# Score matmuls over 128 columns of keys instead of 72 in the cross attention of layer 0

## The reference, cut to what matters

```
q_c = q @ W_dq ;  kv_c = kv @ W_kvc ;  k_rope = rope(kv_c @ W_kr)
scores = (einsum(q_nope, k_nope) + einsum(q_rope, k_rope)) * scale
good = (k_ids <= seg) & (k_ids >= seg - 8)
attn = softmax(where(good, scores, -1e30))
out = einsum(attn, v) @ W_o
```

## Time and profile before

| | before |
|---|---|
| median of 3 runs | 1418.46 us |
| lowest and highest run | 1415.54 and 1429.39 us |
| span of the profiled execution | 1416.6 us |
| PE busy in it | 1114.3 us (79%) |
| weight loads busy | 825.4 us (58%) |
| DVE busy | 764.6 us (54%) |

### The profile page before, as it was taken

The page is one execution under the profiler, slowest core; times in us unless marked ns, Lnnn a source line. Parts: engine busy times, 40 slices in busy tenths (PEclk is TensorE's granted clock), DMA queues, the critical chain, the costliest instruction groups (busy, mean ns, idle before and its releaser), DMA issues.

```text
span 1416.6 us, 14414 instructions
## 1 busy us (share of the span) xinstructions
PE 1114.3 (79%) x5107; PEld 825.4 (58%) x5111; DVE 764.6 (54%) x1025; ACT 469.9 (33%) x719; POOL 479.1 (34%) x331
## 2 busy tenths in 40 slices
PE   3899977879999887686769689699733478489996
PEld 2543454547777766575657678544521367378885
DVE  6212122653344554998999995414697764533333
ACT  2111122552111634464446533333311132133331
POOL 5231212330000433465646560034454980011211
PEclk9799986975555897788878889899955555599999
DMA  6576601220000114313231300102030000111110
GB/s 174 204 266 215 253 0 28 58 60 19 0 0 1 56 42 157 117 47 119 74 106 58 125 10 16 60 0 74 15 121 0 0 0 1 48 60 44 59 44 30
DMA packets 50448, 97.88 MB, mean 69 GB/s; under 512 B 6796, under 2 KB 26564, under 8 KB 47838
## 3 DMA queue, kind: packets, MB, share of 16 engines
q1 hardware_dynamic: 47198, 86.59, 18.4%
q0 software_dynamic: 3200, 10.62, 2.2%
HBM read 96.14 MB, written 1.05 MB: 69 GB/s over the span
## 4 chain that ended last, share of the span: by engine, by line
PE 58%; DVE 23%; issue 11%; ACT 4%; POOL 2%; SPq 0%; DMA 0%; POOLq 0%; DVEq 0%; ACTq 0%
PE banks L41 7%; PE banks L42 7%; PE banks L43 7%; PE banks L354 6%; PE banks L1794 4%; PE banks L1097 3%; PE banks L1096 3%; PE banks L2109 2%; PE banks L1424 2%; PE banks L1452 2%; DVE da_a L1357 1%; PE banks L1087 1%; PE banks L1806 1%; DVE da_s L1351 1%; DVE da_s L1341 1%
## 5 line engine op out<-in xcount | busy, mean ns | idle before, releaser
L155 POOL TENSOR_TENSOR w_low<-w_raw,w_high 128x1024 fp32r<-128x1024 f32 (+2 forms) x66 | 129.9, 1982 | 307.9 <-ACT w_high L151 307.8
L354 PE MATMUL banks<-cs_rows,cs_col 128*2 128x512 f32 x192 | 85.3, 594 | 0.2 <-DVE w_raw L318 0.2
L1642 POOL TENSOR_TENSOR tw_abs<-tw_abs,tw_w 128x2048 bf16<-128x2048 bf16 x12 | 49.0, 4083 | 95.0 <-DVE tw_abs L1635 95.0
L151 ACT CAST w_high<-w_raw 128x1024 fp32r<-128x1024 f32 (+2 forms) x66 | 53.4, 831 | 83.2 <-DMA w_raw<-in_L_attn_Wq 47.1
L2217 POOL TENSOR_TENSOR hf_hl<-hf_h,hf_hh 128x512 fp32r<-128x512 f32 x16 | 20.6, 1289 | 155.1 <-ACT hf_hh L2271 155.1
L1424 PE MATMUL banks<-da_k,da_q 64*128 64x128 f32 x256 | 35.7, 396 | 38.4 <-issue 38.4
L1424 PEld LDWEIGHTS banks<-da_k,da_q 64*128 64x128 f32 x256 | 33.9, 288 | 41.5 <-issue 41.5
L41 PE MATMUL banks<-da_xT_high,w_high 128*128 128x512 f32 x128 | 52.5, 410 | 6.3 <-POOL w_low L155 5.7
L929 DVE SCALAR_TENSOR_TENSOR wa_s<-banks,wa_bd 128x288 f32<-128x288 f32 x16 | 7.3, 457 | 86.4 <-PE banks L1097 86.4
L41 PE MATMUL banks<-hf_xhh,w_high 128*128 128x512 f32 x128 | 51.7, 404 | 0.0
L669 POOL TENSOR_TENSOR wa_kr<-wa_kr,wa_tab 128x288 f32<-128x288 f32 x8 | 6.4, 794 | 132.8 <-ACT wa_kr L724 132.5
(11 more groups left out here) (419 smaller groups left out, 3160.7 us busy)
## 6 DMA issues: line engine op xcount, KB each, us to landing
cs_rows<-in_ctx SPq DMA_DIRECT2D x16, 1536.0 KB
tw_raw<-in_L_ffn_w_gate_up SPq DMA_DIRECT2D x32, 256.0 KB, 3.7
w_raw<-in_L_xattn_W_o SPq DMA_DIRECT2D x8, 512.0 KB
w_raw<-in_L_attn_Wq SPq DMA_DIRECT2D x8, 512.0 KB
w_raw<-in_L_attn_Wk SPq DMA_DIRECT2D x8, 512.0 KB
w_raw<-in_L_attn_Wv SPq DMA_DIRECT2D x8, 512.0 KB
w_raw<-in_L_attn_Wo SPq DMA_DIRECT2D x8, 512.0 KB
tw_raw<-in_L_ffn_w_proj SPq DMA_DIRECT2D x16, 256.0 KB, 3.8
```

What stands on the lines that cost most here:

```text
L151: self.nc.scalar.copy(self.wh[k][:, 0:cols], self.raw[k][:, 0:cols]).then_inc(self.split_hi[k], 1)
L155: self.nc.gpsimd.tensor_tensor(self.wl[k][:, 0:cols], self.raw[k][:, 0:cols], self.wh[k][:, 0:cols].bitcast(F32), ALU.subtract).then_inc(s ...
L354: ins = nc.tensor.matmul(out, self.col[:, h * self.HALF + r, :], self.rows[h][:, r, :], start=(h == 0 and r == 0), stop=False)
L1642: g.tensor_tensor(a, a, self.w[j][:, :], ALU.subtract).then_inc(self.d_ok, 1)
```

## The change

The score matmuls of a group stream 128 columns of keys: the group's own 72 and 56 of its neighbours. For the groups of rounds 0 to 14 the 128 columns begin at the group's own; for the last round, where nothing follows the last group, they end with the group's own (`key_offset` is then 56). A group's result takes 128 columns of the PSUM bank, four groups the whole bank of 512. DVE's first step reads from it the same 4 x 72 columns as before, now with gaps between the groups. All else stays: the number of instructions, the waits, the softmax, both kinds of transposes and the matmuls of L1110.

```
+    def key_offset(r):
+        return 0 if r < WindowAttention.G // 4 - 1 else P - WindowAttention.KEYS
...
-                ch(v.scalar_tensor_tensor(s[:, :, :], c.bank[:, r % 2, 0:4 * self.KEYS].rearrange("p (g k) -> p g k", g=4), X_SCALE,
+                own = slice(self.key_offset(r), self.key_offset(r) + self.KEYS)
+                ch(v.scalar_tensor_tensor(s[:, :, :], c.bank[:, r % 2, :].rearrange("p (g k) -> p g k", g=4)[:, :, own], X_SCALE,
...
+        flat = lambda t: t[:, :, :, :, :].rearrange("p m g j t -> p (m g j t)")
+
+        def wide(t, g):
+            at = g * K8 - self.key_offset(g // 4)
+            return flat(t)[:, at:at + P]
...
-                    out = c.bank[:, n, q * K8:(q + 1) * K8]
-                    nc.tensor.matmul(out, self.qa[:, 8 * g:8 * g + 8, :].rearrange("p t h -> p (t h)"), keys(self.kvcT, g), start=True, stop=False)
-                    ins = nc.tensor.matmul(out, self.qr[:, 8 * g:8 * g + 8, :].rearrange("p t h -> p (t h)"), keys(self.krT, g), start=False, stop=True)
+                    out = c.bank[:, n, q * P:(q + 1) * P]
+                    nc.tensor.matmul(out, self.qa[:, 8 * g:8 * g + 8, :].rearrange("p t h -> p (t h)"), wide(self.kvcT, g), start=True, stop=False)
+                    ins = nc.tensor.matmul(out, self.qr[:, 8 * g:8 * g + 8, :].rearrange("p t h -> p (t h)"), wide(self.krT, g), start=False, stop=True)
```

## The result

The changed kernel takes 1432.17 us at the median of 20 runs (1421.06 to 1444.76), the kernel before 1417.72 us at the median of 20 (1413.45 to 1430.24). The ratio is 1.0081 with a 95% interval of 1.0053 to 1.011: slower, by 7.5 to 15.6 us. Three of the changed kernel's 20 runs (1443.66 us and more) count as slow runs, and the ratio is of the others, whose median is 1429.21 us. The forecast was 1430.4 us, +0.84%, with 1410 to 1440 us as its range.

What follows compares the result with a forecast made beforehand. The score stage's ring of PE scores and DVE's chain was taken as the bound, at clock 0.50. Eight matmuls at 0.0933 us over 16 rounds add 11.9 us: 1418.5 + 11.9 = 1430.4 us, +0.84%, range 1410 to 1440 us.

Steps and rivals of the forecast that it cites:

- The ring: Score stage, each 9.10 us round: L1087 0.86 us, scores 4.88 us, DVE's chain 3.36 us; added score time lengthens all 16 rounds.
- One of two instructions shows its growth: Score matmul pairs: only the second PE instruction's 0.093 us shows; pair 0.63 to 0.73 us, 11.9 us over 16 rounds.
- Charging both instructions: Rival in the score pairs: both instructions show their growth, 23.9 us slower, 1442.4 us; chance 0.04.
- The load waits at a change of rows: Score loop: at each change between 128 and 64 contraction rows, the next load waits for the matmul before it.
- at every change of rows and nowhere else: Argument against 72 columns being slow as a shape: loads start 0.07 us before a matmul's end only at row changes.
- The gapped read costs nothing: DVE's first step, L929: reading 288 elements with gaps stays at 0.46 us; at most 3.6 us more in all.
- The clock stays at 0.50: Score stage: the granted clock stays 0.50 after the change, the stage taking 161 us.
- The rival that wider matmuls lift the clock: Score stage: denser PE streaming restores the full clock; 1382 us if throughout, 1406 us if half; chance 0.11.
- the break-even: Clock rival in the score stage: share of the stage at clock 1.00 that offsets the added columns, put at a quarter.
- Eight changes of rows a round: Score loop: all 8 matmuls of a round have a row change behind them, each showing 0.0933 us, 0.747 us a round.
- The range of 3.6 us for DVE's read: Upper bound for L929's gapped read, as if all 512 elements were read: 0.22 us a round; nothing was taken.
- The doubt whether the result would stand inside or outside 1%: Whole kernel: 11.9 us lies just within the 14.2 us limit; forecast's 0.80 split into 0.58 within and 0.22 slower.

## Why the prediction was right

The forecast rests on the stage, and there sum and rows agree: +11.9 us forecast, 161.59 - 149.66 = 11.9 us measured. That the whole kernel's median came within 2 us of the forecast is in part luck: the profiled execution came out 5.7 us under the span that was forecast (1422.8 against 1428.5 us), and single runs spread over 24 us.

**The ring.** Scores and DVE's chain alternate, and what the scores gain or lose shows in full. DVE's wait for them grew by 11.9 us, PE's idle time stayed at 0.58 us, and the stage grew by 11.9 us. This step held.

**One of two instructions shows its growth.** Predicted 0.72 us a pair and 9.85 us a round, measured 0.72 and 9.85. With 100 columns 9.47 was expected and 9.475 measured. Charging both instructions would have given 23.9 us. Once a pair, then, is shown. Which of the two instructions it is, is not. The prediction says the second, because the next load waits for its end, and this does not fit its own rows: from the second's start to the next load it is 0.35 us with 72 and with 128 columns, and the growth stands before that start, 0.28 us against 0.38 and 0.37 after the change. That the first one's growth hides behind the second load was argued only. Since the ends of matmuls in the trace are modelled, and both instructions of a pair always have the same columns, no run here separates the two. The sum does not depend on it. The Trainium skill's section "Back-to-back issue gap" of the page "TensorE: Matmul & The Clock Gate" would have led to the 23.9 us, since it has the gap follow the moving columns. The same page also says that loads are pulled ahead of running matmuls. The runs agree with that where the rows do not change: 72 columns with 128 rows everywhere step at 0.213 us an instruction, no faster than 128 columns.

**The load waits at a change of rows.** This was read from starts and ends alone, and the runs without changes bear it out by starts alone: at 72 columns a pair falls from 0.63 to 0.43 us. The Trainium skill has a sentence for it, in "TensorEngine Tiling (Array Packing)", section "Key Properties": "Changing tiling mode (not just tile) drains the TensorE". The trace agrees if the step from 128 to 64 rows counts as such a change, and it puts the price at 0.20 us with 72 columns and 0.30 us with 128, at 1.2 GHz. But the prediction's "at every change of rows and nowhere else" is too wide. The step from 128 to 72 rows, from L1102 to L1110, waits for nothing, here in the kernel before:

```profile
390.00 0.63 PE L1102 MATMUL banks<-ident,wa_kvcT 128*72 128x128 f32 x2
390.43 0.85 PE L1110 MATMUL banks<-wa_pt,wa_cn 72*128 72x128 f32 x3
```

Two instructions of L1102 take 0.43 us up to L1110's start, 0.213 each, as within a line. All 186 changes between 128 and 64 rows in that trace between which PE does not pause have the load 0.07 us before the end. A few steps with equal rows have it too, where the weights go between 128 columns and 2 or 8 (L43 to L354, 128 rows in both).

**The gapped read costs nothing.** 0.458 us with gaps, 0.457 without.

**The clock stays at 0.50.** It did, over the whole stage. One reading behind it is off. The prediction puts the clock's fall down to the 6 us in which PE had work for 1.42 us. It fell at their start, at 309.1 us, as their mean of 0.51 says, and in the 6.8 us before that PE was busy for 5.69 us at 1.00:

```profile
302.30:309.10 6.80, 5.69 (x21) 3.29 (x22) 3.25 (x6) 3.40 (x5) 0.75 (x1) 1.00 0.19 74
```

The rival that wider matmuls lift the clock did not happen here. Without row changes it did (0.50 with 72 columns, 0.80 with 128), and with PE's wait filled the changed kernel got the full clock in most of the stage and ran at 0.9879 of the kernel before. So with the row changes the width alone did not bring the clock, and the filling did. The rival's price was put a little too high: rounds at full clock are 7.06 us, not 6.85, because a pair takes 0.42 us, not 0.39. Half of the 0.38 us at the lower clock was too little for the first part, which takes 0.21 us. With 7.06 us the break-even is 27% of the stage at full clock instead of 25%.

**What the argument missed.** Eight changes of rows a round were counted as if alike. For the cost of columns that was right, since the last matmul's length counts whatever follows it (five matmuls showed their growth in the runs with half the changes). For the value of a saved change it was wrong, which showed when four were saved and three paid. The range of 3.6 us for DVE's read was not needed. The doubt whether the result would stand inside or outside 1% was real: the measured 0.81% has an interval that reaches 1.1%.

## What to carry to other kernels

Ask for each matmul what the next load waits for. Where loads are pulled ahead, extra moving columns cost nothing as long as the loads set the pace (at 1.2 GHz 72 and 128 columns both stepped at 0.213 us here). Where the rows of contraction go between 128 and 64 from one matmul to the next, added columns showed once a matmul, 0.093 us for 56 columns, and the change itself cost 0.20 us. Padding the smaller contraction with zeros took 23 us off the stage, with the same instructions. In this stage, which sat at half clock, the clock was the largest price: taking out PE's stalls, widening and then filling PE's wait brought the stage from 149.66 to 97.80 us. Single edits are better judged by the stage's rounds in the trace, because a whole run moves by more than such an edit for reasons elsewhere: two executions here entered the stage 18 us late.

## What the runs showed of the hardware that was not expected

With 128 rows of contraction everywhere and no filling, the stage sat at 0.50 with 72 columns (126.7 us) and at 0.80 with 100 and with 128 (112.0 us both), though at 0.50 the columns alone should have made it slower. That is one profiled execution of each, and why width brings the clock is not shown. And 52 matmuls of the identity, which compute nothing, made the kernel with 128 columns and 128 rows faster by some 14 us in the stage (111.96 to 97.80) by holding the clock.
